# Latent attention: the first four exps of a unit before the rounding of the next q, projections and leaving products half a key tile later

## The chip, the cores and the metric

The kernel is one program on one core of one Trainium2 chip. The metric is the device time of one execution in microseconds (us). A core has a matrix engine (PE, with its weight loads listed as PEld), a vector engine (DVE), a scalar engine for activations (ACT), a general engine (POOL) and a queue for transfers (SP). Each runs its own instructions in order and waits for the others on semaphores.

## The reference, cut to what matters

The program is a stack of four attention and four feed-forward layers on x, 2 x 1024 tokens of 256 features. The change is in the first layer alone:

```python
def _L0_xattn_ref(x, latents, Wq, Wkv, Wo, ln1_w, ln1_b, ln2_w, ln2_b):
    # 16 heads of 64; called with x = context (2 x 77), latents = layernorm(x) (2 x 1024)
    xn = _layernorm(x, ln1_w, ln1_b)
    ln = _layernorm(latents, ln2_w, ln2_b)
    q = ln @ Wq
    k, v = split(concat([xn, ln], axis=-2) @ Wkv)
    logits = einsum('bhld,bhsd->bhls', q * scale, k * scale)
    w = softmax(logits)
    out = einsum('bhls,bhsd->bhld', w, v)
    return out @ Wo
x = x + _L0_xattn_ref(ctx_1024, _layernorm(x), ...)
```

Each of 1024 queries looks at 1024 + 77 = 1101 keys, in 16 heads and 2 batches.

## The kernel before

`latent_attention` works through 16 **units**. A unit n is one pair of heads (two heads of 64 features, index j) in one batch b. Unit n computes its attention and, between its own instructions, prepares unit m = n + 1. `units` lays out the first and the last pair of units by hand and runs the six pairs between in a loop; `body` is called with `first` for unit 0 and `last` for unit 15.

The attention of a unit runs over **key tiles** kt = 0 to 8: eight of 128 keys and one of 77. For each tile and head j, PE makes two **score halves** of 512 queries (`blk`), each as two matmuls (L432 and L434, since q and k are split into a rounded part and a rest). A half has the number 4 kt + 2 j + blk, 0 to 35, and goes to one of three banks, half % 3; from half 3 on PE waits before it until the exp of three halves before has read its bank. ACT makes the exp of each half (L514, `exp_ready`). `values(kt - 1)` (L383) multiplies a finished tile of exps with v after the scores of the next tile; POOL adds the exps up (L621). Behind the last tile PE issues the values of tile 8 and `denominators` (L395), for which ACT waits: it makes logarithm and reciprocal (L527, L530), two table loads among them, and DVE scales the heads (L588). The next unit's first exps come behind these on ACT.

The preparation of unit m shares banks 6, 7 and 3:

- `project_q`, `project_k` (both L309), `project_ctx` (L329, L332) and `project_v` (L341, behind the wait for `k_lo`) on PE. project_q waits for the logarithm, project_k for `x_added`.
- ACT rounds q (`q_hi`, L479), k (`k_hi`, L484) and the context's part (`ctx_copy`), and copies v (`v_copy`, L494). DVE makes the rests (`split_q`, L541, signals `q_lo`; `prepare_k`, L553 and L558, signals `k_lo`) and k_two (L561, `k_second`).
- `maxima`: 48 **pieces**, matmuls of 128 queries by a third of the keys (L355), in a ring of three banks. DVE reduces each (L564, `piece_max`), and PE waits before a piece for the reduction of the piece three before; the first waits for `k_second`, the next two for `v_ready`. After the last, DVE makes the overall maximum (L567, `nmax_ready`), PE transposes it (`rows`, L361), DVE copies it out and SP sends it into q_two (L278, `row_ready`), for which unit m waits at its start.
- `leave(n - 1, c)` (L372) are the **leaving products** of the previous unit: its heads by the output weights, in banks 6 and 7, for feature halves c = 0 and 1. DVE adds each to x (L575, `x_added`). The first waits for the heads and for `q_lo`, since q lies in the same banks until it is split; the second waits for the first add.

The order on each engine is the order of the code. In `body` of PE, `more()` issues the next piece; it is called twice behind each score half and does something from kt = 3 on. In a middle unit PE's order before is: halves 0, 1; project_q; halves 2 to 5; leave c = 0; halves 6, 7; leave c = 1; values 0; halves 8, 9; project_k, project_ctx; halves 10, 11; values 1; project_v; then tiles 3 to 8 with two pieces behind each half and values behind each tile; rows; values 8; denominators. On PE's timeline one f32 matmul of the code is two records, so that x8 of L383 are four.

Of the kernel before, what the change touches and what calls it, by code (L numbers as in the profile page):

```python
# [194 lines left out]
def wait(engine, semaphore, value):  # L195

    if not isinstance(value, int) or value > 0:
        engine.wait_ge(semaphore, value)


def latent_attention(nc, consts, x, a, ctx_n, w_qkv, w_o, t, zeros, slots_zeroed):
# [24 lines left out]
    PIECES = 3 * UNITS  # L226
    with ExitStack() as stack:
# [77 lines left out]
        def _(pe):  # L305
# [7 lines left out]
            def project_q(m, b):  # L313
                if b == 0:
                    pe.wait_ge(s["in_loaded"], 8 * m + 16)
                wait(pe, s["logden_ready"], 2 * m - 2)
                project(0, b).then_inc(s["q_ps"], 1)
# [27 lines left out]
            def maxima(m, b, first, count):  # L345

                for i in range(first, min(first + count, PIECES)):
                    j, qt = divmod(i // 3, QT)
                    if i == 0:
                        pe.wait_ge(s["k_second"], 2 * m + 2)  # L350
                    elif i < 3:
                        pe.wait_ge(s["v_ready"], m + 1)
                    else:
                        pe.wait_ge(s["piece_max"], PIECES * m + i - 2)
                    pe.matmul(ps[:, MAX_BANKS[i % 3], 0:PW], q_one[:, b, j, qt * P:(qt + 1) * P],  # L355
                              k_one[:, b, j, (i % 3) * PIECE:(i % 3) * PIECE + PW], start=True, stop=True)\
                      .then_inc(s["piece_ps"], 1)
# [5 lines left out]
            def leave(n, c, q_after=None):  # L363

                if c == 0:
                    pe.wait_ge(s["heads_ready"], n + 1)
                    if q_after is not None:
                        pe.wait_ge(s["q_lo"], 2 * q_after + 2)
                else:
                    pe.wait_ge(s["x_added"], 2 * n + 1)  # L370
                for blk in range(2):
                    mm = pe.matmul(ps[:, 6 + blk, :], wo[:, c * P:(c + 1) * P], heads[:, blk * BLK:(blk + 1) * BLK],  # L372
                                   start=True, stop=True)
                mm.then_inc(s["y_ps"], 1)
# [32 lines left out]
            def body(n, b, first, last):  # L407
                m, mb = n + 1, 1 - b
                if b == 1:
                    pe.wait_ge(s["out_loaded"], 8 * n + 8)  # L410
                pe.wait_ge(s["row_ready"], 32 * n + 32)
                pe.wait_ge(s["k_second"], 2 * n + 2)
                done = 0

                def more():

                    nonlocal done
                    if not last and kt >= 3 and done < PIECES:
                        maxima(m, mb, done, 1)
                        done += 1  # L420

                for kt in range(KT):
                    kw = P if kt < KT - 1 else CTX
                    for j in range(2):
                        for blk in range(2):
                            cols = slice(blk * BLK, (blk + 1) * BLK)
                            half = 4 * kt + 2 * j + blk
                            if half >= 3:
                                pe.wait_ge(s["exp_ready"], 4 * KT * n + half - 2)
                            else:  # L430
                                wait(pe, s["exp_ready"], 4 * KT * n)
                            pe.matmul(ps[0:kw, half % 3, :], k_one[:, b, j, kt * P:kt * P + kw], q_one[:, b, j, cols],  # L432
                                      start=True, stop=False)
                            pe.matmul(ps[0:kw, half % 3, :], k_two[:, b, j, kt * P:kt * P + kw], q_two[:, b, j, cols],  # L434
                                      start=False, stop=True).then_inc(s["score_ps"], 1)
                            more()
                            more()
                        if (kt, j) == (0, 0) and not last:
                            project_q(m, mb)
                        if kt == 1 and not first:  # L440
                            leave(n - 1, j, None if last else m)
                        if (kt, j) == (2, 0) and not last:
                            project_k(m, mb)
                            project_ctx(m, mb)
                        if j and kt:
                            values(n, b, kt - 1)
                        if (kt, j) == (2, 1) and not last:
                            project_v(m, mb)
                if not last:
                    kt = KT  # L450
                    while done < PIECES:
                        more()
                    rows(m)
                values(n, b, KT - 1)
                if last:
                    pe.wait_ge(s["x_added"], 2 * n)
                denominators(n)
                if last:
                    leave_last(n)
# [14 lines left out]
        @block.scalar  # L474
        def _(act):
            def q_hi(m, b):
                act.wait_ge(s["q_ps"], m + 1)
                for j in range(2):
                    act.activation(q_one[OWN[j], b, j, :], bank_pair(6)[OWN[j]], ACT.Copy).then_inc(s["q_hi"], 1)  # L479

            def k_hi(m, b):
                act.wait_ge(s["k_ps"], m + 1)
                for j in range(2):
                    act.activation(k_one[OWN[j], b, j, 0:S], bank_pair(6)[OWN[j]], ACT.Copy).then_inc(s["k_hi"], 1)  # L484

            def ctx_copy(m, b):
                act.wait_ge(s["ctx_ps"], m + 1)
                for j in range(2):
                    act.activation(k_one[OWN[j], b, j, S:KEYS], ps[OWN[j], 3, 0:CTX], ACT.Copy).then_inc(s["ctx_hi"], 1)
                act.activation(v_tok[0:CTX, b, KT - 1, :], ps[0:CTX, 3, P:2 * P], ACT.Copy).then_inc(s["ctx_v"], 1)  # L490

            def v_copy(m, b):
                act.wait_ge(s["v_ps"], m + 1)
                act.activation(v_tok[:, b, 0:KT - 1, :], ps[:, 6:8, :].rearrange("p b (t n) -> p (b t) n", n=P),  # L494
                               ACT.Copy).then_inc(s["v_ready"], 1)

            def prologue(m, b):
                q_hi(m, b)
                k_hi(m, b)
                ctx_copy(m, b)  # L500
                v_copy(m, b)

            def body(n, b, first, last):
                m, mb = n + 1, 1 - b
                for kt in range(KT):
                    kw = P if kt < KT - 1 else CTX
                    for j in range(2):
                        if kt >= RING:
                            act.wait_ge(s["pv_ps"], KT * n + kt - RING + 1)
                            act.wait_ge(s["summed"], 2 * (KT - 1) * n + 2 * max(kt - RING, 1))  # L510
                        for blk in range(2):
                            half = 4 * kt + 2 * j + blk
                            act.wait_ge(s["score_ps"], 4 * KT * n + half + 1)
                            act.activation(probs[0:kw, j, kt % RING, blk * BLK:(blk + 1) * BLK], ps[0:kw, half % 3, :],  # L514
                                           ACT.Exp, scale=1.0 / 8.0).then_inc(s["exp_ready"], 1)
                        if last:
                            continue
                        if (kt, j) == (0, 0):
                            q_hi(m, mb)
                        if (kt, j) == (2, 0):  # L520
                            k_hi(m, mb)
                            ctx_copy(m, mb)
                        if (kt, j) == (2, 1):
                            v_copy(m, mb)
                act.wait_ge(s["den_ps"], n + 1)
                for blk in range(2):
                    act.activation(logden[:, blk * BLK:(blk + 1) * BLK], ps[:, DEN_BANKS[blk], :],  # L527
                                   ACT.Ln).then_inc(s["logden_ready"], 1)
                act.wait_ge(s["logden_ready"], 2 * n + 2)
                act.activation(rden[:, :], logden[:, :], ACT.Exp, scale=-1.0).then_inc(s["rden_ready"], 1)  # L530

            act.wait_ge(s["zeroed"], 7)
            units(act, body, prologue)
# [2098 lines left out]
```

## Time and profile before

| | |
|---|---|
| median of 3 runs | 3894.61 us (3887.56 to 3901.64) |
| profiled execution, its own time | 3885.98 us |
| its span, first to last instruction | 3883.9 us |
| granted TensorE clock, mean of the span | 0.882 |
| PE busy | 2982.6 us, 77% |
| DVE busy | 2169.9 us, 56% |
| ACT busy | 1530.2 us, 39% |
| POOL busy | 1070.8 us, 28% |
| latent attention, first score to last output (141.9 to 1183.4 us) | 1041.5 us, 27% of the span |

Times inside the trace count from the first instruction. A row of a timeline has the start, the time, engine, line of the code, operation, what it writes and reads, and how many such instructions the row merges; in brackets stands how long the engine was idle before and who ended that. The ends of matmuls are modelled, and the next may be issued before: two score matmuls follow each other every 0.23 us though each is listed with 0.39. So distances between starts say more than the listed times. Idle time in brackets counts from the modelled end, and is shorter than the wait.

### The profile page before, as it was taken

To read this page: it belongs to the slowest core of one execution; us is meant where nothing else is said; L and a number is where in the kernel's file an instruction comes from. 1 tells how busy PE (TensorE), PEld (TensorE's weight loads), DVE (VectorE), ACT (ScalarE), POOL (GpSimd) and SP (SyncE) were. 2 spreads that over 40 slices of the span, in tenths; PEclk is the share of its full clock that TensorE was granted. 3 is DMA by queue.
4 is the path that set the end of the run, shared out by engine and by line. 5 is a ranking of instruction groups with operands and counts; after the bars stand their busy time and mean duration, and the time that the engine had idled before them with its cause. 6 is when DMAs were issued, how large, how long until landed. Compare 5 with 4: busy or idle time off the path is not lost. (4 is left out here: it accounts for less than half of the span.)

```text
span 3883.9 us, 42386 instructions
## 1 busy us (share of the span) xinstructions
PE 2982.6 (77%) x14406; PEld 1812.9 (47%) x14406; DVE 2169.9 (56%) x4032; ACT 1530.2 (39%) x2131; POOL 1070.8 (28%) x628
## 2 busy tenths in 40 slices
PE   4899999999994668629968599999728971039989
PEld 1545454545442545329945243333228960014457
DVE  3646565555532437238827278888427846863366
ACT  2344444444441423416623335555605631012254
POOL 1356565656571313043303100000052311001100
PEclk7899999999996789759989779999958996569999
DMA  3020000000021410036510000000025631010150
GB/s 71 5 58 12 6 5 2 4 6 5 2 64 38 143 59 1 2 127 218 194 60 1 11 2 3 5 4 2 1 69 195 219 107 19 1 24 17 38 217 22
DMA packets 86631, 198.02 MB, mean 51 GB/s; under 512 B 19923, under 2 KB 62291, under 8 KB 78416
## 3 DMA queue, kind: packets, MB, share of 16 engines
q0 software_dynamic: 18480, 108.86, 7.8%
q1 hardware_dynamic: 64144, 83.24, 7.1%
q10 hardware_dynamic: 3856, 3.95, 0.5%
q8 instruction: 90, 1.47, 0.2%
q14 instruction: 61, 0.50, 0.0%
HBM read 145.99 MB, written 49.76 MB: 50 GB/s over the span
## 5 line engine op out<-in xcount | busy, mean ns | idle before, releaser
L621 POOL TENSOR_TENSOR A_key_sums<-A_key_sums,A_probs 128x1024 f32<-128x1024 f32 (+1 forms) x224 | 526.6, 2370 | 228.1 <-ACT A_probs L514 228.1
L514 ACT ACTIVATE A_probs<-A_banks 128x512 f32<-128x512 f32 (+1 forms) x576 | 329.1, 597 | 385.9 <-PE A_banks L434 383.7
L564 DVE TENSOR_REDUCE A_part_max<-A_banks 128x1 f32<-128x367 f32 x768 | 354.0, 531 | 157.1 <-PE A_banks L355 155.6
L1814 DVE TENSOR_REDUCE F_part_max<-F_banks 128x1 f32<-128x512 f32 x512 | 324.9, 683 | 58.6 <-PE F_banks L1667 55.7
L1760 ACT ACTIVATE F_probs<-F_banks 128x1024 f32<-128x1024 f32 x256 | 248.0, 1022 | 237.3 <-PE F_banks L1713 237.1
L383 PE MATMUL A_banks<-A_probs,A_v_tok 128*64 128x512 f32 x1152 | 278.7, 605 | 0.0
L432 PE MATMUL A_banks<-A_q_one,A_k_one 128*128 128x512 f32 (+1 forms) x576 | 256.4, 445 | 26.3 <-ACT A_probs L514 23.2
L355 PE MATMUL A_banks<-A_k_one,A_q_one 128*128 128x368 f32 x768 | 230.0, 382 | 6.8 <-ACT A_v_tok L494 6.4
L434 PE MATMUL A_banks<-A_q_two,A_k_two 128*128 128x512 f32 (+1 forms) x576 | 227.5, 395 | 0.0
L184 POOL TENSOR_SCALAR F_r<-F_r,F_ln_w 128x512 f32<-128x512 f32 x16 | 28.8, 1812 | 657.0 <-DVE F_r L149 657.0
L355 PEld LDWEIGHTS A_banks<-A_k_one,A_q_one 128*128 128x128 f32 x768 | 147.3, 192 | 94.9 <-DVE A_part_max L564 58.6
L2092 PE MATMUL G_banks<-G_path_rows,G_ctx_hi 77*128 77x512 f32 x8 | 5.2, 649 | 224.8 <-DMA G_path_rows<-align_path 224.8
L432 PEld LDWEIGHTS A_banks<-A_q_one,A_k_one 128*128 128x128 f32 (+1 forms) x576 | 106.3, 185 | 139.3 <-issue 97.5
L1667 PE MATMUL F_banks<-F_k_split,F_q_split 64*128 64x512 f32 x512 | 156.7, 489 | 7.0 <-DVE F_part_max L1814 5.2
L2253 POOL TENSOR_TENSOR H_diff<-H_logits 128x512 f32<-128x512 f32 x32 | 40.7, 1272 | 423.0 <-DVE H_logits L2229 417.4
L621 POOL TENSOR_TENSOR A_key_sums<-A_probs 128x1024 f32<-128x1024 f32 x32 | 75.9, 2374 | 262.1 <-ACT A_probs L514 262.1
L1680 PE MATMUL F_banks<-F_probs,F_v_tok 128*32 128x512 f32 x1024 | 143.2, 632 | 1.6 <-ACT F_probs L1760 1.5
L309 PE MATMUL A_banks<-g_y,A_wqkv 128*128 128x512 f32 x256 | 120.7, 616 | 30.6 <-DVE A_part_max L604 26.0
L879 PE MATMUL F_banks<-F_y_hi,F_w_split 128*128 128x256 f32 x736 | 129.4, 289 | 14.2 <-DVE F_w_split L1068 14.2
L879 PE MATMUL D_banks<-D_y_hi,D_w_split 128*128 128x256 f32 x736 | 128.9, 288 | 14.0 <-DVE D_w_split L1068 14.0
L1713 PE MATMUL F_banks<-F_q_split,F_k_split 64*128 64x512 f32 x512 | 131.0, 463 | 7.0 <-ACT F_probs L1760 5.8
L1667 PEld LDWEIGHTS F_banks<-F_k_split,F_q_split 64*128 64x128 f32 x512 | 71.8, 196 | 134.0 <-DVE F_part_max L1814 106.4
(567 smaller groups left out, 6542.3 us busy)
## 6 DMA issues: line engine op xcount, KB each, us to landing
Hm_staged<-in_H_w SPq DMA_DIRECT2D x6, 1024.0 KB, 5.2
moe_in_D<-A_zeros SPq DMA_DIRECT2D x1, 6003.0 KB, 27.0
moe_in_F<-A_zeros SPq DMA_DIRECT2D x1, 6003.0 KB, 26.1
D_tile_in<-moe_in_D SPq DMA_DIRECT2D x23, 261.0 KB, 5.8
F_tile_in<-moe_in_F SPq DMA_DIRECT2D x23, 261.0 KB, 5.2
H_phi<-in_H_w SPq DMA_DIRECT2D x5, 1024.0 KB, 5.4
H_w<-in_H_w SPq DMA_DIRECT2D x5, 1024.0 KB, 6.2
D_y_tok<-moe_out_D SPq DMA_DIRECT2D x8, 512.0 KB, 5.3
```

What stands on the lines that cost most here:

```text
L355: pe.matmul(ps[:, MAX_BANKS[i % 3], 0:PW], q_one[:, b, j, qt * P:(qt + 1) * P], k_one[:, b, j, (i % 3) * PIECE:(i % 3) * PIECE + PW], star ...
L383: mm = pe.matmul(ps[DH * j:DH * j + DH, 4 + blk, :], v_tok[:, b, kt, DH * j:DH * j + DH], probs[:, j, kt % RING, blk * BLK:(blk + 1) * BLK ...
L432: pe.matmul(ps[0:kw, half % 3, :], k_one[:, b, j, kt * P:kt * P + kw], q_one[:, b, j, cols], start=True, stop=False)
L434: pe.matmul(ps[0:kw, half % 3, :], k_two[:, b, j, kt * P:kt * P + kw], q_two[:, b, j, cols], start=False, stop=True).then_inc(s["score_ps" ...
L514: act.activation(probs[0:kw, j, kt % RING, blk * BLK:(blk + 1) * BLK], ps[0:kw, half % 3, :], ACT.Exp, scale=1.0 / 8.0).then_inc(s["exp_re ...
L564: dve.tensor_reduce(part_max[:, i // 3, i % 3:i % 3 + 1], ps[:, MAX_BANKS[i % 3], 0:PIECE], AX.X, ALU.max).then_inc(s["piece_max"], 1)
L621: pool.tensor_tensor(key_sums[0:kw, j, :], before, probs[0:kw, j, kt % RING, :], ALU.add).then_inc(s["summed"], 1)
L879: mm = pe.matmul(ps[:, 1 + pairs * (n % 2) + pair, at * SLOT:(at + 1) * SLOT], weight_in(i, w_part, pair, c, QM * q + at), part[:, i % 2, ...
L1667: mm = pe.matmul(bank, q_split[rr, b, qt * P // BLK, hd // 2, qt * P % BLK:qt * P % BLK + P], k_split[rr, b, hd // 2, kb * BLK:(kb + 1) * ...
L1680: mm = pe.matmul(ps[V0 * hd:V0 * hd + V0, 7, :], v_tok[:, b, kt, V0 * hd:V0 * hd + V0], probs[:, i % RING, hd, :], start=kt == 0, stop=kt ...
L1760: act.activation(probs[:, i % RING, heads_at, :], ps[:, heads_at, :], ACT.Exp, scale=DH ** -0.5).then_inc(s["exp_ready"], 1)
L1814: op = dve.tensor_reduce(part_max[:, maximum_at(hd, qt), kb:kb + 1], bank, AX.X, ALU.max)
```

## The change

Four places in `body` of PE and three in `body` of ACT:

- ACT makes exps 0 to 3 before `q_hi`, where it made exps 0 and 1 before.
- `k_hi` and `ctx_copy` come after exp 11 (before: after exp 9), `v_copy` after exp 13 (before: 11).
- The leaving products come after values 0 (c = 0) and after halves 8 and 9 (c = 1). Before they came after halves 4, 5 and 6, 7.
- project_k and project_ctx come after halves 10, 11, and so ahead of values 1; project_v after halves 12, 13.
- Pieces of the maxima begin with head j = 1 of tile 3: the condition `kt >= 3` becomes `2 * kt + j >= 7`. What is left of the 48 pieces when the tiles are done is issued by the loop that already stood ahead of `rows`.

```diff
@@ -415,7 +415,7 @@
                 def more():
 
                     nonlocal done
-                    if not last and kt >= 3 and done < PIECES:
+                    if not last and 2 * kt + j >= 7 and done < PIECES:
                         maxima(m, mb, done, 1)
                         done += 1
 
@@ -437,14 +437,16 @@
                             more()
                         if (kt, j) == (0, 0) and not last:
                             project_q(m, mb)
-                        if kt == 1 and not first:
-                            leave(n - 1, j, None if last else m)
-                        if (kt, j) == (2, 0) and not last:
+                        if (kt, j) == (2, 0) and not first:
+                            leave(n - 1, 1)
+                        if (kt, j) == (2, 1) and not last:
                             project_k(m, mb)
                             project_ctx(m, mb)
                         if j and kt:
                             values(n, b, kt - 1)
-                        if (kt, j) == (2, 1) and not last:
+                        if (kt, j) == (1, 1) and not first:
+                            leave(n - 1, 0, None if last else m)
+                        if (kt, j) == (3, 0) and not last:
                             project_v(m, mb)
                 if not last:
                     kt = KT
@@ -515,12 +517,12 @@
                                            ACT.Exp, scale=1.0 / 8.0).then_inc(s["exp_ready"], 1)
                         if last:
                             continue
-                        if (kt, j) == (0, 0):
+                        if (kt, j) == (0, 1):
                             q_hi(m, mb)
-                        if (kt, j) == (2, 0):
+                        if (kt, j) == (2, 1):
                             k_hi(m, mb)
                             ctx_copy(m, mb)
-                        if (kt, j) == (2, 1):
+                        if (kt, j) == (3, 0):
                             v_copy(m, mb)
                 act.wait_ge(s["den_ps"], n + 1)
                 for blk in range(2):
```

No instruction is added or removed on ACT, DVE or POOL, and no waits of other kinds.

PE, head of the second unit (L372 leaving products, L383 values of tile 0):

```order
 L432 MATMUL A_banks<-A_q_one,A_k_one 128x512
 L434 MATMUL A_banks<-A_q_two,A_k_two 128x512
+L432 MATMUL A_banks<-A_q_one,A_k_one 128x512
+L434 MATMUL A_banks<-A_q_two,A_k_two 128x512
+L432 MATMUL A_banks<-A_q_one,A_k_one 128x512
+L434 MATMUL A_banks<-A_q_two,A_k_two 128x512
+L383 MATMUL A_banks<-A_probs,A_v_tok 64x512 x4
 L372 MATMUL A_banks<-A_heads,A_wo 128x512 x2
 L432 MATMUL A_banks<-A_q_one,A_k_one 128x512
...
 L434 MATMUL A_banks<-A_q_two,A_k_two 128x512
 L372 MATMUL A_banks<-A_heads,A_wo 128x512 x2
-L383 MATMUL A_banks<-A_probs,A_v_tok 64x512 x4
 L432 MATMUL A_banks<-A_q_one,A_k_one 128x512
 L434 MATMUL A_banks<-A_q_two,A_k_two 128x512
```

Halves 6 and 7 and the values of tile 0 now stand ahead of the first leaving product, and halves 8 and 9 between the two.

ACT, head of the second unit, before (L514 exps, L479 q_hi, L484 k_hi, L489 and L490 ctx_copy, L494 v_copy):

```order
L514 ACTIVATE A_probs<-A_banks 128x512 x2
L479 ACTIVATE A_q_one<-A_banks 64x1024 x2
L514 ACTIVATE A_probs<-A_banks 128x512 x8
L484 ACTIVATE A_k_one<-A_banks 64x1024 x2
L489 ACTIVATE A_k_one<-A_banks 64x77 x2
L490 ACTIVATE A_v_tok<-A_banks 77x128
L514 ACTIVATE A_probs<-A_banks 128x512 x2
L494 ACTIVATE A_v_tok<-A_banks 128x1024
L514 ACTIVATE A_probs<-A_banks 128x512 x20
```

and now, with each line number two higher:

```order
L516 ACTIVATE A_probs<-A_banks 128x512 x4
L481 ACTIVATE A_q_one<-A_banks 64x1024 x2
L516 ACTIVATE A_probs<-A_banks 128x512 x8
L486 ACTIVATE A_k_one<-A_banks 64x1024 x2
L491 ACTIVATE A_k_one<-A_banks 64x77 x2
L492 ACTIVATE A_v_tok<-A_banks 77x128
L516 ACTIVATE A_probs<-A_banks 128x512 x2
L496 ACTIVATE A_v_tok<-A_banks 128x1024
L516 ACTIVATE A_probs<-A_banks 128x512 x18
```

Two exps moved from behind q_hi to ahead of it, and with them k_hi, ctx_copy and v_copy stand two exps further back.

PE, tile 3 of the second unit, from the context's projections on (L341 project_v, L355 pieces):

```order
 L329 MATMUL A_banks<-A_ctx_n,A_wqkv 128x77 x2
 L332 MATMUL A_banks<-A_wqkv,A_ctx_n 77x128 x2
...
+L383 MATMUL A_banks<-A_probs,A_v_tok 64x512 x4
...
 L341 MATMUL A_banks<-A_wqkv,g_y 128x128 x16
-L432 MATMUL A_banks<-A_q_one,A_k_one 128x512
-L434 MATMUL A_banks<-A_q_two,A_k_two 128x512
-L355 MATMUL A_banks<-A_k_one,A_q_one 128x368 x2
-L432 MATMUL A_banks<-A_q_one,A_k_one 128x512
-L434 MATMUL A_banks<-A_q_two,A_k_two 128x512
-L355 MATMUL A_banks<-A_k_one,A_q_one 128x368 x2
```

The values of tile 1 stand ahead of halves 12 and 13, and the four pieces that stood behind these halves are gone from here.

PE, tail of the second unit (L361 rows):

```order
 L355 MATMUL A_banks<-A_k_one,A_q_one 128x368 x2
 L383 MATMUL A_banks<-A_probs,A_v_tok 64x512 x4
+L355 MATMUL A_banks<-A_k_one,A_q_one 128x368 x4
 L361 MATMUL A_banks<-g_ident,A_nmax 16x128
 L383 MATMUL A_banks<-A_probs,A_v_tok 64x512 x4
```

Four pieces now stand behind the values of tile 7, directly ahead of the transposition.

## Rows read from the trace of the kernel before

**Rows 1.** The page's first line: the span of the profiled execution.
```profile
span 3883.9 us, 42386 instructions
```

**Rows 2.** Windows of units: length, busy us (x instructions) per engine, PEclk, DMA share, GB/s.
```profile
268.31:333.54 65.23, 62.94 (x268) 33.92 (x266) 36.62 (x63) 30.94 (x49) 37.65 (x16) 1.00 0.42 103
333.54:1115.69 782.15, 754.45 (x3183) 407.01 (x3180) 439.34 (x756) 371.30 (x588) 451.84 (x192) 1.00 0.01 4
```

**Rows 3.** Timeline of PE, head: start us, us, instruction, xcount, [idle before <-releaser].
```profile
275.62 0.39 PE L434 MATMUL A_banks<-A_q_two,A_k_two 128*128 128x512 f32 x1
...
276.08 0.40 PE L434 MATMUL A_banks<-A_q_two,A_k_two 128*128 128x512 f32 x1
277.86 0.50 PE L432 MATMUL A_banks<-A_q_one,A_k_one 128*128 128x512 f32 x1 [1.38 <-ACT A_probs L514]
...
278.70 1.98 PE L372 MATMUL A_banks<-A_heads,A_wo 128*128 128x512 f32 x4
...
282.00 1.98 PE L372 MATMUL A_banks<-A_heads,A_wo 128*128 128x512 f32 x4 [0.38 <-DVE g_x L575]
283.92 1.94 PE L383 MATMUL A_banks<-A_probs,A_v_tok 128*64 128x512 f32 x8
...
286.83 3.60 PE L309 MATMUL A_banks<-g_y,A_wqkv 128*128 128x512 f32 x8
...
294.04 3.84 PE L341 MATMUL A_banks<-A_wqkv,g_y 128*128 128x128 f32 x32
...
298.99 0.44 PE L355 MATMUL A_banks<-A_k_one,A_q_one 128*128 128x368 f32 x1 [0.35 <-ACT A_v_tok L494]
...
301.96 1.94 PE L383 MATMUL A_banks<-A_probs,A_v_tok 128*64 128x512 f32 x8
```

**Rows 4.** Timeline of ACT in the same unit's head.
```profile
273.61 1.06 ACT L514 ACTIVATE A_probs<-A_banks 128x512 f32<-128x512 f32 x2
275.12 2.06 ACT L479 ACTIVATE A_q_one<-A_banks 64x1024 fp32r<-64x1024 f32 x2 [0.45 <-PE A_banks L309]
277.21 2.06 ACT L514 ACTIVATE A_probs<-A_banks 128x512 f32<-128x512 f32 x4
...
290.46 2.06 ACT L484 ACTIVATE A_k_one<-A_banks 64x1024 fp32r<-64x1024 f32 x2 [2.81 <-PE A_banks L309]
```

**Rows 5.** Timeline of DVE in the same unit's head.
```profile
276.17 2.48 DVE L541 TENSOR_TENSOR A_q_two<-A_banks,A_q_one 64x1024 fp32r<-64x1024 f32 x2 [1.22 <-ACT A_q_one L479]
...
284.02 1.22 DVE L575 TENSOR_TENSOR g_x<-g_x,A_banks 128x1024 f32<-128x1024 f32 x1 [2.08 <-PE A_banks L372]
...
291.51 2.48 DVE L553 TENSOR_TENSOR A_k_one<-A_banks,A_k_one 64x1024 fp32r<-64x1024 f32 x2 [4.82 <-ACT A_k_one L484]
```

**Rows 6.** Timeline of PE at the same unit's tail.
```profile
329.69 1.94 PE L383 MATMUL A_banks<-A_probs,A_v_tok 128*64 128x512 f32 x8
331.56 0.28 PE L361 MATMUL A_banks<-g_ident,A_nmax 128*16 128x128 f32 x1
...
335.35 0.50 PE L432 MATMUL A_banks<-A_q_one,A_k_one 128*128 128x512 f32 x1
```

**Rows 7.** Timeline: PE's first maximum, then the reductions of DVE.
```profile
298.21 0.43 PE L355 MATMUL A_banks<-A_k_one,A_q_one 128*128 128x368 f32 x1
...
298.68 0.54 DVE L564 TENSOR_REDUCE A_part_max<-A_banks 128x1 f32<-128x367 f32 x1 [0.53 <-PE A_banks L355]
...
326.95 3.66 DVE L564 TENSOR_REDUCE A_part_max<-A_banks 128x1 f32<-128x367 f32 x8 [1.85 <-PE A_banks L355]
330.65 0.20 DVE L567 TENSOR_REDUCE A_nmax<-A_part_max 128x16 f32<-128x48 f32 x1
```

**Rows 8.** Window of the second unit's head, columns as in rows 2.
```profile
211.50:216.84 5.34, 5.14 (x11) 2.46 (x11) 2.01 (x2) 1.84 (x4) 2.34 (x1) 0.68 0.00 0
```

**Rows 9.** Timeline of the last unit: PE behind its first wait, POOL's last sums.
```profile
1121.62 0.50 PE L432 MATMUL A_banks<-A_q_one,A_k_one 128*128 128x512 f32 x1 [2.46 <-ACT A_probs L514]
...
1132.05 32.63 POOL L621 TENSOR_TENSOR A_key_sums<-A_key_sums,A_probs 128x1024 f32<-128x1024 f32 x14 [3.01 <-ACT A_probs L514]
```

## The prediction

> **What bounds the kernel now.** The profiled execution spans 3883.9 us [rows 1]; its own time is 3885.98 us, so 2 us lie around the span, and the median of the three timed runs, 3894.61 us, is 8.6 us above it. I work on the trace and add the difference to that median. The change touches latent attention alone, 16 units long. First I read the windows of its units [rows 2]: the unit from 268.31 takes 65.23 us, and the next twelve 782.15 us, 65.18 each. PE is busy 62.94 us of 65.23, DVE 36.62, ACT 30.94, POOL 37.65, at a granted clock of 1.00. So PE is the bound, and a unit grows by whatever PE waits more. Then I read PE's own timeline at the two ends of a unit, and beside it ACT and DVE.
>
> At the head [rows 3 to 5] ACT is late, since it made the previous unit's reciprocals: it runs exps 0 and 1 from 273.61, then q_hi from 275.12, and exps 2 to 5 from 277.21. PE has finished issuing score half 4 by 276.31 (the L434 at 276.08 and 0.23 more; halves come 0.46 apart) and waits until 277.86, 1.55 us, for exp 2 to free a bank. It waits again for the split q before the first leaving product (278.70), and 0.38 us in its row for DVE's add before the second (282.00), which always starts 3.30 after the first.
>
> At the tail [rows 6] there is no wait: values of key tile 7 run from 329.69, and the transposition of the maxima (L361) follows 1.87 later, at 331.56, exactly as long as eight such products take. DVE's last reductions end at 330.61 and the overall maximum at 330.85 [rows 7], both under those values. The next unit begins at 335.35, 3.79 after L361.
>
> **The tail: four maxima without cover.** The old rule puts 8 pieces into each of 6 key tiles, 48. The new one begins half a tile later and leaves 44; the last four come after the values of tile 7. PE gets there at 331.56. A maximum's first reduction starts 0.47 after the matmul (298.21 and 298.68 in [rows 7]), so at 332.03; eight reductions take 3.66, four 1.83: 333.86. The overall maximum starts 0.04 later and takes 0.20 [rows 7]: 334.10. PE follows DVE by 0.05 (splits end at 291.51 + 2.48 = 293.99 in [rows 5], PE starts at 294.04 in [rows 3]): L361 at 334.15. That is +2.59 us. Behind L361 on PE stand the values of tile 8 and the denominators, for which ACT, then the next unit's head wait; nothing passes it. The four matmuls lie within these 2.59: the first three have banks free, the fourth waits for the first reduction only. The DMA of the rows starts later by the same amount as its user, so its slack stays.
>
> **The head: one wait for another.** ACT now runs exps 2 and 3 before q_hi. Score half 3 is written at 275.62 + 0.39 = 276.01, its exp follows at about 276.05 and passes in 0.52 (four take 2.06), so q_hi starts at 276.6, 1.5 late, and ends its 2.09 (275.12 to 277.21) at 278.7. On PE halves 5 and 6 need exps 2 and 3 and now run at once, from 276.31 to 277.23: the old wait of 1.55 is gone. But half 7 needs exp 4, which stands behind q_hi. Before, PE started 0.65 after the exp behind q_hi did (277.21 to 277.86); now that is 279.35. A new wait of 2.1 us. Half 7 (0.6) and values of tile 0 (1.87) bring the first leaving product to 281.85; the split q is ready by then (DVE ends it 3.53 after q_hi starts: 275.12, and 276.17 + 2.48), so that wait goes. The second comes 3.30 later, at 285.15, its add ends 3.24 after that (284.02 + 1.22 against 282.00), and project_k, which writes the same banks, starts at 288.45. PE is ready for it at about 288.0 (1.92 for the products, 282.00 to 283.92, and two halves), so this is a small new wait of 0.4. Against 286.83 project_k is 1.6 late.
>
> From there the chain is what it was: k_hi 3.63 behind project_k [rows 4], the splits, project_v. PE has the same work between the two projections, two halves and one values, so project_v moves from 294.04 to 295.65 and the second maximum, released by v_copy, from 298.99 to 300.6. Behind it stood three halves with maxima before the values of tile 2 (301.96); now stands one. A half is worth 0.9 (two reductions, 3.66 / 4), so 300.6 + 2.97 - 1.8 = 301.8. The head gains 0.2 us in all.
>
> The later tiles keep their 5.55 each (301.96 to 329.69 is five). POOL's sums start with the exps and get a little more slack; k_hi, ctx_copy and v_copy move behind exps whose scores are long there, at no cost, since PE reaches the banks later anyway. SP's loads of weights wait for v_ps and y_ps, 1.6 to 3 us later in a unit of 65: hidden; if that cover were gone, it would be these 3 us.
>
> **The sum.** 2.59 - 0.2 = 2.4 us per unit that looks ahead. There are 15 of them: the first has no leaving products, but the same wait behind q_hi and the same four maxima. 15 x 2.4 = 36. The last unit has no look-ahead. It ends on POOL: 14 sums back to back in 32.63 us from 1132.05 [rows 9]. PE restarts there at 1121.62; five halves, values, the first leaving product, two halves and an exp give sum 3 at about 1129.5 and, with the second leaving product at 1129.3, exps 11 and 13 at 1132.9 and 1135.75. Sum 5 started at 1132.05 + 2 x 2.33 = 1136.7, now 1135.75: -1. Together +35 us.
>
> **The clock.** This term is not settled by a wait. In the second unit the same head took 5.34 us from 211.50 to 216.84 at a mean granted clock of 0.68, where the next unit took 4.14 (277.86 to 282.00) at 1.00 [rows 2, 3, 8]: 1.2 us for one fall to 1.2 GHz, behind the 1.4 us wait and the wait for the split. It happened once: the thirteen units behind it ran at 1.00 [rows 2]. The wait of 2.46 us in the last unit [rows 9] went without one. The change makes two longer idle stretches per unit, 2.1 at the head and 2.6 with four short matmuls in it at the tail: 30 places. Bounds: none falls, 0, or all, 36 us. I take six, nearer to the rows of before, +7.
>
> So +42 on 3894.6: 3937 us.
>
> **A rule that speaks against the change.** The Trainium skill, TensorE: Matmul & The Clock Gate, section "A second HAM failure mode: psum-queue depth-cycling", says that short waits between groups of matmuls, each small, can make the clock swing between its two levels and cost throughput. By the rows alone a short wait is harmless 13 times in 14 and the sum stays near +35; by the rule nearly each of the 30 places pays. The trace of before supports it once. It is the second rival below.
>
> **Rivals.**
> *The clock falls at nearly every new wait*: 30 x 1.2 = 36 on top of 35, 3966 us. For it: one fall in the second unit after less idle time. Against: thirteen heads and the 2.46 us wait without one.
> *The head runs free (the other side).* If exps 0 to 3 ahead of q_hi freed PE's banks so early that half 7, the second leaving product and project_k never waited, the head would give back 2.1 + 0.46 + 0.45 = 3.0 us more per unit, since v_copy and the maxima follow project_k. (0.46 is 3.30 less 1.92 for the products and 0.92 for two halves.) Then a unit has 2.4 - 3.0 = -0.6, in all -10: 3885 us, about at the bound of what can be told from no change; if the tail is 0.2 cheaper too, 3882. It decides at 2.4 us given back. Against it: exp 4 stands behind both halves of q_hi on the same engine [rows 4], and the add is a fixed 3.30.
> *Only the wait at half 7 vanishes*, because exp 4's bank is not what PE needs: 2.4 - 2.1 = 0.3 per unit, +4: 3898 us, no difference.
> *The change doesn't do what it says*: excluded by the listing of the instructions, where exps, leaving products and four maxima stand where the code puts them.
>
> **How the numbers follow.** The forecast, both ends of a unit as worked out and few clock falls: 0.72. Clock falls nearly everywhere: 0.18. Head free: 0.05, of which 0.03 beyond the bound. Half 7 free, no difference: 0.05. A measurement of this kernel can tell about 0.3%, 12 us, from no change; so faster 0.03, same 0.07, slower 0.90. The range reaches down to no clock fall and one us per unit less (3930 - 15) and up to the clock rival with its highest price: 3915 to 3970.
>
> **What would show it.** On PE: a wait of about 2.1 us for an exp at the fourth score half behind project_q, none before it; L361 behind a wait for the overall maximum, some 4.5 us after the values of tile 7 began; units of 67.6 us; no maxima in the first half of tile 3. On ACT: four exps, then q_hi. On DVE: four reductions after the values of tile 7. The granted clock of a unit below 1.00 would price the third term. The forecast is wrong if units stay at 65.2, which would mean that the tail is covered, or if half 7 doesn't wait.

## The result

The changed kernel takes 3938.77 us (median of 4, 3934.37 to 3944.22), the kernel before beside it 3891.09 us. The ratio is 1.0122, 95% interval 1.0098 to 1.0146: 47.7 us slower. The forecast was 3937 us, +42. The profiled execution spans 3933.8 us, 49.9 more than before.

The first lines of the page of the changed kernel, which answer to [rows 1]:

```profile
span 3933.8 us, 42386 instructions
## 1 busy us (share of the span) xinstructions
PE 3001.6 (76%) x14406; PEld 1819.8 (46%) x14406; DVE 2202.7 (56%) x4032; ACT 1529.8 (39%) x2131; POOL 1072.4 (27%) x628
```

The same instructions, as many as before. The windows of three units in a row, each from one transposition of the maxima (L361) to the next, columns as in [rows 2]:

```profile
271.75:341.07 69.32, 64.82 (x265) 34.26 (x265) 38.69 (x63) 30.94 (x49) 37.79 (x16) 0.98 0.38 97
341.07:408.79 67.72, 63.18 (x265) 33.84 (x265) 38.68 (x63) 30.82 (x49) 37.84 (x16) 1.00 0.00 1
408.79:476.51 67.72, 63.19 (x266) 33.84 (x266) 38.69 (x63) 30.84 (x49) 37.77 (x16) 1.00 0.02 8
```

A unit takes 67.72 us where it took 65.18, and some take 69.32. PE is busy nearly as long as before (63.18 of them, 62.94 in [rows 2]), so 2.3 of the 2.5 us are idle time. The 1.6 us more of the first window come with a granted clock of 0.98, not 1.00. From the first L361 to the last, 15 units, the sum is 1024.7 us against 975.25.

**Tail.** PE at the end of a unit, and DVE beside it; these answer to [rows 6] and [rows 7]:

```profile
404.28 1.94 PE L383 MATMUL A_banks<-A_probs,A_v_tok 128*64 128x512 f32 x8
406.15 0.77 PE L355 MATMUL A_banks<-A_k_one,A_q_one 128*128 128x368 f32 x3
407.21 0.43 PE L355 MATMUL A_banks<-A_k_one,A_q_one 128*128 128x368 f32 x1 [0.30 <-DVE A_part_max L566]
408.79 0.28 PE L361 MATMUL A_banks<-g_ident,A_nmax 128*16 128x128 f32 x1 [1.15 <-DVE A_nmax L569]
```

```profile
406.62 1.88 DVE L566 TENSOR_REDUCE A_part_max<-A_banks 128x1 f32<-128x367 f32 x4 [1.42 <-PE A_banks L355]
408.53 0.20 DVE L569 TENSOR_REDUCE A_nmax<-A_part_max 128x16 f32<-128x48 f32 x1
```

The values of tile 7 start at 404.28; 1.87 later come three pieces at once, 406.15, a wait of 0.30 for the first reduction, the fourth, and a wait for DVE's overall maximum (L569, which was L567). The transposition follows 4.51 behind the start of the values, where it was 1.87: 2.64 us, forecast 2.59.

**Head.** The same unit goes on, to be held against [rows 3]:

```profile
418.07 0.39 PE L434 MATMUL A_banks<-A_q_two,A_k_two 128*128 128x512 f32 x1
...
419.51 0.40 PE L434 MATMUL A_banks<-A_q_two,A_k_two 128*128 128x512 f32 x1
421.74 0.50 PE L432 MATMUL A_banks<-A_q_one,A_k_one 128*128 128x512 f32 x1 [1.83 <-ACT A_probs L516]
...
422.41 1.94 PE L383 MATMUL A_banks<-A_probs,A_v_tok 128*64 128x512 f32 x8
424.27 1.98 PE L372 MATMUL A_banks<-A_heads,A_wo 128*128 128x512 f32 x4
...
427.57 1.98 PE L372 MATMUL A_banks<-A_heads,A_wo 128*128 128x512 f32 x4 [0.38 <-DVE g_x L577]
...
430.87 3.70 PE L309 MATMUL A_banks<-g_y,A_wqkv 128*128 128x512 f32 x8 [0.40 <-DVE g_x L577]
...
443.14 0.44 PE L355 MATMUL A_banks<-A_k_one,A_q_one 128*128 128x368 f32 x1 [0.42 <-ACT A_v_tok L496]
...
444.30 1.94 PE L383 MATMUL A_banks<-A_probs,A_v_tok 128*64 128x512 f32 x8
```

and ACT, against [rows 4]:

```profile
416.06 1.06 ACT L516 ACTIVATE A_probs<-A_banks 128x512 f32<-128x512 f32 x2
418.04 1.09 ACT L516 ACTIVATE A_probs<-A_banks 128x512 f32<-128x512 f32 x2 [0.91 <-PE A_banks L434]
419.01 2.06 ACT L481 ACTIVATE A_q_one<-A_banks 64x1024 fp32r<-64x1024 f32 x2
421.09 2.07 ACT L516 ACTIVATE A_probs<-A_banks 128x512 f32<-128x512 f32 x4
```

Four exps stand ahead of q_hi now, which starts at 419.01, and the old wait at half 5 is gone: halves 5 and 6 run through. Half 7 waits from 419.74 (the L434 at 419.51 and 0.23) to 421.74, 2.0 us, for the exp that ACT starts at 421.09 behind q_hi. The first leaving product has no wait, the second stands 3.30 behind it, and project_k (430.87) waits 0.40 in its row for the add. From L361 to project_k it is 22.08 us; before, in the unit of [rows 3], 286.83 - 266.34 = 20.49 (L361 of that unit at 266.34). That is +1.6, as forecast. The second piece of the maxima stands 34.35 behind L361 (443.14) where it was 32.65 (298.99), +1.70, and the values of tile 2 follow at 35.51 (444.30) where they were at 35.62 (301.96): tile 3, with one half instead of three between these two, gives 1.81 back, and the head comes out 0.11 shorter.

**Clock.** A **fall** is here a drop of the granted clock to 1.2 GHz. A unit with a fall, from the restart of half 7 to the first leaving product, and the same stretch of the unit above:

```profile
284.70:288.84 4.14, 4.14 (x11) 1.22 (x11) 0.79 (x1) 1.52 (x3) 3.63 (x2) 0.59 1.06 248
421.74:424.27 2.53, 2.53 (x10) 0.78 (x10) 0.79 (x1) 1.42 (x3) 2.02 (x1) 1.00 0.00 0
```

4.14 against 2.53: 1.6 us for one fall, as much as the whole unit is longer (69.32 against 67.72). In the 15 units there are seven, six of them in heads and one behind a transposition; before there was one. The last column but two is PEclk.

### The profile page after: what moved, and what is told of

It reads as the page before. It is cut to its first block and busy times, and to the rows that moved or that the text cites. A ratio compares the mean times of both kernels' runs of the same rounds, so it can differ in the third digit from the quotient of the medians.

```text
span 3933.8 us, 42386 instructions
## 1 busy us (share of the span) xinstructions
PE 3001.6 (76%) x14406; PEld 1819.8 (46%) x14406; DVE 2202.7 (56%) x4032; ACT 1529.8 (39%) x2131; POOL 1072.4 (27%) x628
## 5 line engine op out<-in xcount | busy, mean ns | idle before, releaser
L383 PE MATMUL A_banks<-A_probs,A_v_tok 128*64 128x512 f32 x1152 | 287.8, 622 | 0.0
L355 PE MATMUL A_banks<-A_k_one,A_q_one 128*128 128x368 f32 x768 | 229.5, 382 | 12.0 <-ACT A_v_tok L496 7.2
L434 PE MATMUL A_banks<-A_q_two,A_k_two 128*128 128x512 f32 (+1 forms) x576 | 229.5, 398 | 0.0
L355 PEld LDWEIGHTS A_banks<-A_k_one,A_q_one 128*128 128x128 f32 x768 | 146.0, 192 | 108.6 <-DVE A_part_max L566 61.3
```

The lines of the kernel that those rows point to most:

```text
L383: mm = pe.matmul(ps[DH * j:DH * j + DH, 4 + blk, :], v_tok[:, b, kt, DH * j:DH * j + DH], probs[:, j, kt % RING, blk * BLK:(blk + 1) * BLK ...
```

## The experiments

Every experiment lists units without a fall (from L361 to L361) and its falls in the 15 units that look ahead, read from its trace. Comparisons are with the kernel before run beside it on the same chip, its median 3887 to 3891 us. Falls are those of the one traced execution, and another execution of the same kernel may have more or fewer: the traced one of e9 took 3924.71 us at a mean clock of 0.883 over the whole program, its other three 3934.68 to 3937.33 us at 0.879 to 0.881. So a difference of two or three falls between two kernels says little.

| kernel | unit without fall, us | falls at head / tail | median, us | ratio to before, interval |
|---|---|---|---|---|
| before | 65.18 | 1 / 0 | | 1 |
| changed | 67.72 | 6 / 1 | 3938.77 | 1.0122 (1.0098, 1.0146) |
| e1_tail_covered | 65.78 | 7 / 0 | 3899.99 | 1.0032 (1.0018, 1.0047) |
| e2_tail_only | 66.33 | 2 / 5 | 3917.56 | 1.0080 (1.0063, 1.0097) |
| e3_old_q_hi | 67.27 | 0 / 3 | 3922.09 | 1.0091 (1.0074, 1.0107) |
| e4_new_q_hi_only | 66.57 | 13 / 0 | 3930.03 | 1.0111 (1.0094, 1.0127) |
| e5_spread | 63.54 | 2 / 0 | 3867.31 | 0.9938 (0.9924, 0.9951) |
| e6_spread_order | 63.21 | 0 / 0 | 3858.16 | 0.9919 (0.9905, 0.9933) |
| e7_filled_head | 69.05 | 0 / 6 | 3953.67 | 1.0167 (1.0153, 1.0182) |
| e8_order | 64.84 | 0 / 0 | 3882.25 | 0.9982 (0.9973, 0.9991) |
| e9_filled_half | 67.72 | 0 / 4 | 3935.95 | 1.0126 (1.0108, 1.0145) |

The theory was the forecast's: four pieces without cover at the tail cost 2.6 us a unit, the head trades a wait for another and gives little, and the clock adds a few falls. The rival was that the head's new wait is what costs.

### e1_tail_covered: the changed kernel, four pieces behind values

```diff
                         if j and kt:
                             values(n, b, kt - 1)
+                            if 4 <= kt < 8:
+                                more()
```

> The changed kernel, but with one more piece of the maxima behind the values of tiles 3 to 6, where DVE is idle for 1.9 us, so that no piece is left for the tail. Theory (four uncovered pieces cost 2.6 us a unit, the head nothing much): the transposition follows the values of tile 7 after 1.87 us again, a unit without a clock fall takes 65.2 to 65.8 instead of 67.72, clock falls stay at some heads (the 2.1 us wait is still there); in all 3898 to 3910 us, -30 to -40 against the changed kernel. Rival (the head's new wait for exp 4 is the cost): units stay above 67, no gain beyond 5 us.

Measured 3899.99 us, 38.8 below the changed kernel. PE at the tail of a unit:

```profile
330.30 1.94 PE L383 MATMUL A_banks<-A_probs,A_v_tok 128*64 128x512 f32 x8
332.16 0.28 PE L361 MATMUL A_banks<-g_ident,A_nmax 128*16 128x128 f32 x1
```

The transposition is 1.86 behind the values again, the unit 65.78. The four pieces cost 0.7 us where DVE is idle, and 2.64 at the tail. The head is untouched here, with its wait of 1.83 in the row, and keeps falling, seven times. The rival falls: head and tail can be told apart, and without the tail only 0.6 us a unit and the clock are left of the loss.

### e2_tail_only: the kernel before, pieces half a tile later

```diff
-                    if not last and kt >= 3 and done < PIECES:
+                    if not last and 2 * kt + j >= 7 and done < PIECES:
```

> The kernel before with one line changed: pieces begin half a tile later (2 * kt + j >= 7). Theory: the tail costs the same +2.6 as in the changed kernel (transposition 4.5 us behind the start of the values of tile 7), of which 1.6 come back in tile 3, where halves 12 and 13 run without pieces and without waits on DVE; units of 66.2 to 66.5, +15 to +20 us against before. Clock: heads unchanged, so falls at most once or twice. Rival (head): units stay at 65.2.

Units of 66.33, as expected: 2.64 lost, 1.5 won back in tile 3. The total is a miss, +27 us where I expected 15 to 20. The difference is the clock: I had written of the heads alone, and the tail itself makes it fall. PE behind the wait at the tail, and the window with its clock:

```profile
331.72 0.77 PE L355 MATMUL A_banks<-A_k_one,A_q_one 128*128 128x368 f32 x3
332.78 0.43 PE L355 MATMUL A_banks<-A_k_one,A_q_one 128*128 128x368 f32 x1 [0.29 <-DVE A_part_max L564]
334.36 0.28 PE L361 MATMUL A_banks<-g_ident,A_nmax 128*16 128x128 f32 x1 [1.15 <-DVE A_nmax L567]
334.57 3.57 PE L383 MATMUL A_banks<-A_probs,A_v_tok 128*64 128x512 f32 x8
```

```profile
334.47:338.00 3.53, 3.53 (x11) 1.01 (x12) 0.28 (x1) 0.00 (x0) 0.00 (x0) 0.54 0.01 2
```

Eight records of values take 3.57 us instead of 1.94 at a clock of 0.54.

### e3_old_q_hi: the changed kernel, q_hi back behind exp 1

```diff
-                        if (kt, j) == (0, 1):
+                        if (kt, j) == (0, 0):
                             q_hi(m, mb)
```

> The changed kernel with q_hi back behind exps 0 and 1. Theory: the wait of 2.1 us at score half 7 goes and the old one of 1.5 us at half 5 comes back; from there on everything 0.6 earlier, units of 67.1 to 67.2 instead of 67.72 and fewer clock falls at the head; -8 to -16 us against the changed kernel. Rival (exps ahead of q_hi pay): units longer than 67.72. Rival (the wait's place is indifferent): 67.72.

Units of 67.27, 0.45 shorter, and 16.7 us less than the changed kernel, both just outside what I expected. Score half 5 waits 1.36 to 1.39 in its row again instead of 1.83 at half 7, and no head falls any more; three tails do. So the four exps ahead of q_hi cost, they don't pay: 15 x 0.45 = 7 us by the wait, and about as much by the clock (three falls instead of seven, at 1.6 to 1.7 us). The 3 us that are left of the 16.7 are within the spread of the runs.

### e4_new_q_hi_only: the kernel before, q_hi behind exp 3

```diff
-                        if (kt, j) == (0, 0):
+                        if (kt, j) == (0, 1):
                             q_hi(m, mb)
```

> The kernel before with q_hi alone moved behind exps 2 and 3, leaving products in their old place. Theory: the first leaving product stands behind half 5 and waits for the split q, 3.53 us behind q_hi, so it starts 1.5 later than before (280.2 instead of 278.70 in the unit shown) and the whole unit with it: units of 66.7, +22 us and clock falls at some heads. Rival (the exps let PE run on, the split is not in the way): units of 65.2 or less.

Units of 66.57, 0.13 less than expected, but +39.6 us in all where I expected 22. PE at the head of a unit:

```profile
278.65 0.40 PE L434 MATMUL A_banks<-A_q_two,A_k_two 128*128 128x512 f32 x1
282.21 1.13 PE L372 MATMUL A_banks<-A_heads,A_wo 128*128 128x512 f32 x2 [3.16 <-DVE A_q_two L541]
```

One wait of 3.3 us (3.16 in the row) ahead of the first leaving product, which waits for the split q. The window from there to the second leaving product in this unit, without a fall, and in the next, with one:

```profile
282.21:285.51 3.30, 2.90 (x8) 1.44 (x8) 1.22 (x1) 0.81 (x2) 2.02 (x1) 1.00 1.08 282
348.79:353.78 4.99, 4.60 (x8) 2.02 (x8) 1.22 (x1) 0.82 (x2) 2.01 (x1) 0.66 0.00 0
```

3.30 against 4.99, 1.7 us. The transfers in the first of these windows (282 GB/s) don't make the fall: the window with the fall has none. It falls in 13 of the 14 units that have this wait (the first has no leaving products), some 22 us, as much as the wait itself (15 x 1.4 = 21).

The unit lengths of before, e2, e3 and changed add up one part at a time: the later pieces +1.15 (65.18 to 66.33), the later leaving products and projections +0.94 (to 67.27), the four exps +0.45 (to 67.72). These are prices in that order, not of each part by itself: the four exps alone cost +1.39 in e4, where the first leaving product stands right behind them and waits for the split q.

### e7_filled_head and e9_filled_half: matmuls in the wait

```diff
                             half = 4 * kt + 2 * j + blk
+                            if half == 7 and not last:
+                                for c in range(4):
+                                    pe.matmul(ps[:, 3, :], wqkv[:, 0, c % C, :], a[:, c % C, 0:BLK], start=True, stop=True)
```

> The changed kernel with four more f32 matmuls of 512 columns, whose results nobody reads, in bank 3 ahead of score half 7, where PE waits 2.1 us for exp 4; they take 4 x 0.43 = 1.72 us of that wait. Theory (the clock falls come from PE's idle time in that wait): units without a fall stay at 67.72, the falls at the heads go (five units of 69.3 become 67.7), -6 to -10 us against the changed kernel. Rival (the falls have another cause, or the added work counts on the path): falls stay, or units grow by up to 1.7.

I mis-sized the filler: one such f32 matmul is two records 0.43 apart, so four take 3.44 us and overrun the wait by 1.33, which is just what the units grow (69.05). So it takes 3953.67 us, 15 more than the changed kernel, where I expected 6 to 10 less. The falls at heads are gone, and, not expected, six stand at tails, where the changed kernel had one. e9 takes `range(2)`:

> e7_filled_head with two added matmuls instead of four. There each was twice as long as I had put it (eight passes of 0.43 in 3.44 us, 1.33 more than the wait holds, and units of 69.05). Two take 1.72 us and fit into the 2.1 us. Theory: units without a fall are 67.72 again, no fall at a head, some (two to five) at the tail, where PE still waits for the overall maximum; 3932 to 3942 us, within a few us of the changed kernel. Rival (the added work costs beyond the wait): units above 67.9. Rival (idle time at the head isn't what makes the clock fall there): falls at heads as in the changed kernel.

PE in a unit of e9, the filler (L430) and half 7 (L435) behind it, which no longer shows a wait:

```profile
348.56 1.88 PE L430 MATMUL A_banks<-g_y,A_wqkv 128*128 128x512 f32 x4
350.55 0.50 PE L435 MATMUL A_banks<-A_q_one,A_k_one 128*128 128x512 f32 x1
```

Half 7 stands 12.95 behind L361 (337.60), exactly as without the filler (421.74 - 408.79). The windows behind two transpositions, one with a fall and one without:

```profile
405.29:411.20 5.91, 5.91 (x19) 1.93 (x20) 0.28 (x1) 0.30 (x1) 0.00 (x0) 0.71 0.01 1
337.60:341.40 3.80, 3.80 (x18) 1.16 (x18) 0.28 (x1) 0.00 (x0) 0.00 (x0) 1.00 0.01 2
```

The first window reaches 0.4 us into the next unit; to the same instruction, the next unit's first half, it is 5.49 against 3.79, 1.7 us for the fall.

Units of 67.72 again, no fall at a head, four at tails, 3935.95 us: the filler is free, and PE's idle time in that wait is what makes the head fall (none of 15 against six). But filling one wait gives little in the end, since the other falls instead: the 15 traced units are 4.6 us shorter for three falls less, and the medians are 2.8 us apart, which the spread of the runs doesn't tell from nothing. Why the tail falls more often when the head doesn't, and whether it does so in every execution, isn't settled by these runs.

### e8_order, e5_spread, e6_spread_order: a faster kernel

```diff
-                        if kt == 1 and not first:
-                            leave(n - 1, j, None if last else m)
+                        if (kt, j) == (1, 1) and not first:
+                            leave(n - 1, 0, None if last else m)
...
                             values(n, b, kt - 1)
+                        if (kt, j) == (1, 1) and not first:
+                            leave(n - 1, 1)
```

> The kernel before with the leaving products alone in the place of e6_spread_order. Theory: -0.5 us a unit, 64.6 to 64.8 instead of 65.17, -6 to -9 us. Rival: 65.17.

Units of 64.84 and -5.7 us, each just short of what I put (64.6 to 64.8, -6 to -9): the values of tile 0 between the leaving products cover the wait for the first add. The fall of the kernel before isn't there either.

```diff
                             more()
-                            more()
+                            if blk or kt == KT - 1:
+                                more()
...
                             values(n, b, kt - 1)
+                            if kt < KT - 1:
+                                more()
+                                more()
```

> The kernel before, with the same 48 pieces of the maxima in the same tiles, but spread: in tiles 3 to 7 one, two, one, two pieces behind the four score halves and two behind the values, where DVE is idle for 1.9 us; in tile 8 two behind each half as before. Theory: two reductions (0.91 us) are longer than a half with two pieces on PE (0.79), so PE waits about 0.1 for DVE in most halves; spread, these waits go and a tile takes 5.2 instead of 5.55 us. Units of 63.2 to 63.6 instead of 65.2, -23 to -30 us. Rival (PE is bound by its own issue, DVE's releases are hidden): units of 65.2, no difference.

Units of 63.54, as expected, and -20.6 us, short of the 23. PE through a tile of e6_spread_order, which has the same pieces:

```profile
305.73 1.94 PE L383 MATMUL A_banks<-A_probs,A_v_tok 128*64 128x512 f32 x8
307.60 0.60 PE L355 MATMUL A_banks<-A_k_one,A_q_one 128*128 128x368 f32 x2
308.04 0.39 PE L432 MATMUL A_banks<-A_q_one,A_k_one 128*128 128x512 f32 x1
308.27 0.40 PE L434 MATMUL A_banks<-A_q_two,A_k_two 128*128 128x512 f32 x1
308.50 0.33 PE L355 MATMUL A_banks<-A_k_one,A_q_one 128*128 128x368 f32 x1
308.67 0.39 PE L432 MATMUL A_banks<-A_q_one,A_k_one 128*128 128x512 f32 x1
...
310.99 1.51 PE L383 MATMUL A_banks<-A_probs,A_v_tok 128*64 128x512 f32 x6
```

From values to values it is 5.26 us, in the kernel before 5.55 (301.96 to 329.69 in [rows 3, 6], five tiles). The two pieces behind the values (307.60) are reduced while PE is at the next half; then one, two, one, two leave DVE time. Three in four of PE's waits for a reduction, which its weight loads show, are gone. Between 263 and 1082 us, before and in e6_spread_order (us in total, times, longest):

```profile
PEld A_banks L355 <- DVE A_part_max L564: 40.7, 206, 0.2
PEld A_banks L355 <- DVE A_part_max L570: 10.4, 52, 0.2
```

The rival, that these waits were hidden, falls.

> As e5_spread, and the first leaving product after halves 6 and 7, then the values of tile 0, then the second leaving product. Theory: the wait for the split q and the one for DVE's first add get cover, 0.5 us a unit on top of e5_spread: units of 62.7 to 63.1, -30 to -38 us against before, and at most a few clock falls. Rival (the leaving products' place is indifferent): as e5_spread.

Both together: units of 63.21 and -29.8 us, just short of what I expected (63.1 at most, -30 to -38), no fall, 3858.16 us, 0.8% faster than before and 2.0% faster than the changed kernel.

## Why the prediction was right

- **The bound.** PE's waits set the unit: its busy time hardly moved (62.94 to 63.18) and the unit grew by 2.54. Right, and e1, e3 and e9 each move the unit by what PE waits less, e9 by nothing where the filler fits in the wait.
- **Tail, 2.59.** Measured 2.64. Worked out from two rows of DVE and one of PE [rows 6, 7]; e1 takes it away and e2 makes it alone.
- **Head, -0.2.** Half 7's new wait, the missing wait before the first leaving product, the 3.30 between the two and the small wait before project_k are all there, and project_k is 1.6 late. The head gives 0.11 a unit. The working had 0.16 (301.8 against 301.96), rounded to 0.2: what comes back in tile 3 is its 1.8, but the second piece is 1.70 late, not 1.61. 2.64 less 0.11 is, but for rounding, the 2.54 by which a unit grew, and 15 times 0.14 more than forecast is 2 us.
- **The last unit, -1.** Wrong by 1.9 up to POOL's last sums: the fifth sum, from which POOL runs without a break, begins 15.96 us behind PE's restart (1183.99 - 1168.03). Before it was 15.1 (1136.7 - 1121.62), forecast 14.1. A clock fall, which the forecast didn't have there, slowed the halves that feed it: from 1168.86 on score matmuls come 0.43 apart instead of 0.23. PE, then POOL:

```profile
1168.03 0.50 PE L432 MATMUL A_banks<-A_q_one,A_k_one 128*128 128x512 f32 x1 [2.44 <-ACT A_probs L516]
...
1168.60 0.47 PE L432 MATMUL A_banks<-A_q_one,A_k_one 128*128 128x512 f32 x1
1168.86 0.63 PE L434 MATMUL A_banks<-A_q_two,A_k_two 128*128 128x512 f32 x1
1169.29 0.63 PE L432 MATMUL A_banks<-A_q_one,A_k_one 128*128 128x512 f32 x1
```

```profile
1183.99 27.96 POOL L623 TENSOR_TENSOR A_key_sums<-A_key_sums,A_probs 128x1024 f32<-128x1024 f32 x12 [0.71 <-ACT A_probs L516]
```

The whole last unit is 2.0 us shorter all the same: from its L361 to its last add 67.65 (1160.12 to 1227.77) against 69.69 (1113.71 to 1183.40). Its closing products ran at the lower clock before and at the higher one now; here are the second four records, before and changed. The forecast had none of this, so that -2.0 lies near its -1 is luck.

```profile
1178.37 3.78 PE L467 MATMUL A_banks<-A_heads,A_wo 128*128 128x512 f32 x4 [1.31 <-DVE g_x L575]
1224.53 1.98 PE L469 MATMUL A_banks<-A_heads,A_wo 128*128 128x512 f32 x4 [1.31 <-DVE g_x L577]
```

- **The clock, +7.** The one term without a row of its own, and that its count came out is luck: there are six falls more than before, seven instead of one, and I took six, but no row gave that number. Their price was too low, 1.6 to 1.7 each instead of 1.2, perhaps since the fall of before lay partly over other waits: some 10 us instead of 7. One argument for few falls was weak: the last unit's wait of 2.46 us, which passed without a fall before, stands in all eleven traces (2.44 to 2.46 in the row), and in six of them a fall begins within 1.5 us behind it.
- **The balance.** The 15 units came out at +49.4 in the trace: 38 of waiting, 10 of falls and, by difference, 1.2 in the first unit. Its first score ran at 138.88 instead of 141.91, while the low clock of the start ended at 144.8 in both, so it had 3 us more at 1.2 GHz. The whole span grew by nearly the same 49.9 only because other stretches cancel: the first L361 is 3.0 us earlier, the last unit 2.0 shorter, and what follows latent attention 5.5 longer, none of it forecast or followed up.
- **Rivals.** No free head: exp 4 stood behind q_hi, and the add stayed at 3.30. "The clock falls at nearly every new wait" wasn't the case for this change (7 of 30 places), but e4 shows that it can be: 13 of the 14 units with its long wait. The Trainium skill, TensorE: Matmul & The Clock Gate, "A second HAM failure mode: psum-queue depth-cycling", says that short waits between groups of matmuls can make the clock swing. These traces agree: at the heads, waits of 2.0 to 3.3 us do it in 6 to 13 units of 15, waits of 1.5 us in none to two. At an uncovered tail, where PE waits 0.3 and 1.15 us in the rows with one piece between, it happens in one to six.

## What to carry to other kernels

Where one engine runs without gaps and another follows it piece by piece, what is pushed out at the end of a stretch stands without cover: count the pieces (48 slots became 44) and price what is left by the follower's rate, not by the engine's. Work that needs a slower partner goes where that partner is idle: the same pieces behind the values cost 0.7 us instead of 2.64, and spread evenly they made the kernel faster than it had been. Before moving an engine's work ahead of a step, ask who waits for the steps now behind it; here four early exps saved a wait of 1.5 us and made one of 2.0.

## What I had not expected of the hardware

- A wait of PE can cost more than its length: a fall to 1.2 GHz behind it took 1.6 to 1.7 us more. In e4 that doubled the loss.
- With one wait filled, the falls stood at another (heads 6 to 0, tails 1 to 4, one trace each), and little was gained: 3935.95 against 3938.77 us.
- Nearly all falls stand alone, and a kernel with long waits in each unit still falls in a part of them only (7 of 15 heads in e1, every second unit from the fourth on; every third in the changed kernel). What picks the unit isn't settled.
